# Reciprocals of the softmax row sums spread over partitions through a DRAM row, in an attention and soft-mixture kernel

## What is computed

```python
q = (x @ Wq).reshape(B, N, HEADS, DIM_HEAD)          # x: [8, 56, 128], layer-normed
k = (context @ Wk).reshape(B, M, HEADS, DIM_HEAD)    # context: [8, 1500, 128]
v = (context @ Wv).reshape(B, M, HEADS, DIM_HEAD)
attn = softmax(einsum('bihd,bjhd->bhij', q, k) * SCALE)
x = x + einsum('bhij,bjhd->bihd', attn, v).reshape(B, N, INNER) @ Wo
# then, on layernorm(x):
logits = (einsum('tzd,ed->tze', x, phi_w) + phi_b).reshape(t, z, n, p)
D, C = softmax(logits, axis=3), softmax(logits, axis=2)
X_tilde = tanh(norm(clip(einsum('tznp,tzd->npd', D, x))))
Y_tilde = einsum('npd,ndH->npH', X_tilde, expert_w) + expert_b
out = x + einsum('tznp,npH->tzH', C, Y_tilde)
```

## Time and profile before

| | |
|---|---|
| three runs | 484.78, 487.85, 488.55 us; median 487.85 us |
| profiled execution | span 483.5 us from its first to its last instruction; no other time of it is given |
| PE busy | 441.9 us (91%), weight loads 384.6 us (80%) |
| DVE busy | 359.2 us (74%) |
| ACT busy | 256.8 us (53%) |
| POOL busy | 120.6 us (25%) |
| chain that ended last | PE 69%, DVE 22%, DMA 4%, ACT 3% of the span |

### The profile page before, as it was taken

How to read it: one execution, slowest core, us unless ns; L and a number is a source line. 1 busy time by engine, 2 the same in 40 slices (tenths; PEclk the granted TensorE clock), 3 DMA queues, 4 the chain that set the end, 5 groups by cost and what they waited for, 6 DMA issues and landing times.

```text
span 483.5 us, 7391 instructions
## 1 busy us (share of the span) xinstructions
PE 441.9 (91%) x2776; PEld 384.6 (80%) x2776; DVE 359.2 (74%) x600; ACT 256.8 (53%) x439; POOL 120.6 (25%) x55
## 2 busy tenths in 40 slices
PE   2899899999999999999999999999999995865767
PEld 2788788898899889988988897889878875565657
DVE  2467776777786777768666877675799999999780
ACT  1466566665564556656565565663666640325532
POOL 0507000503050022305000503050123428434250
PEclk9999999999999999999999999999999999778899
DMA  7110100010010001000100021000000009800000
GB/s 214 42 64 1 66 1 0 1 65 0 2 42 24 1 0 66 0 0 2 61 0 0 30 85 37 1 1 1 0 2 0 1 0 276 159 0 2 1 1 20
DMA packets 8496, 15.38 MB, mean 32 GB/s; under 512 B 291, under 2 KB 4275, under 8 KB 8469
## 3 DMA queue, kind: packets, MB, share of 16 engines
q1 hardware_dynamic: 6996, 12.91, 9.2%
q10 hardware_dynamic: 1472, 2.10, 1.5%
HBM read 14.78 MB, written 0.23 MB: 31 GB/s over the span
## 4 chain that ended last, share of the span: by engine, by line
PE 69%; DVE 22%; DMA 4%; ACT 3%; issue 1%; POOL 0%; SPq 0%; DVEq 0%
PE turned L575 14%; PE scores L563 7%; PE scores L565 7%; PE scores L564 7%; PE acc L593 7%; PE acc L595 7%; PE acc L594 7%; DVE csum L1359 3%; PE misc L507 3%; DMA ctx_raw<-in_ctx_dram 3%; DVE bankmax L1290 3%; DVE cmax L1342 2%; DVE pT_l L1299 2%; PE misc L609 2%; PE misc L501 2%; DVE disp L1377 2%
## 5 line engine op out<-in xcount | busy, mean ns | idle before, releaser
L1299 DVE TENSOR_TENSOR pT_l<-turned,pT_h 125x512 fp32r<-125x512 f32 x168 | 112.2, 688 | 65.8 <-ACT pT_h L1019 65.3
L1019 ACT CAST pT_h<-turned 125x512 fp32r<-125x512 f32 x168 | 95.3, 592 | 112.6 <-PE turned L575 112.4
L1290 DVE TENSOR_REDUCE bankmax<-scores 128x1 f32<-128x500 f32 x168 | 110.5, 675 | 20.6 <-PE scores L565 20.3
L575 PEld LDWEIGHTS turned<-ident,prob 128*125 128x125 f32 x672 | 88.3, 187 | 14.7 <-DVE pT_l L1299 8.5
L575 PE MATMUL turned<-ident,prob 128*125 128x128 f32 x672 | 94.4, 276 | 2.4 <-DVE pT_l L1299 2.2
L1026 ACT ACTIVATE prob<-scores,negmax 128x1500 f32<-128x1500 f32 x56 | 85.1, 1520 | 9.9 <-DVE negmax L1293 9.8
L593 PE MATMUL acc<-pT_h,ctx_nh 125*128 125x384 f32 (+1 forms) x192 | 78.2, 407 | 0.0
L595 PE MATMUL acc<-pT_h,ctx_nl 125*128 125x384 f32 (+1 forms) x192 | 70.1, 365 | 0.0
L594 PE MATMUL acc<-pT_l,ctx_nh 125*128 125x384 f32 (+1 forms) x192 | 69.9, 364 | 0.0
L563 PE MATMUL scores<-ctx_th,qk_h 128*128 128x500 f32 x168 | 69.2, 412 | 0.6 <-DVE qk_l L1283 0.3
L385 POOL TENSOR_TENSOR ctx_nh<-ctx_raw,zero 125x1536 fp32r<-125x1536 f32 x8 | 22.0, 2748 | 184.4 <-PE acc L595 169.3
(11 more groups left out here) (169 smaller groups left out, 581.1 us busy)
## 6 DMA issues: line engine op xcount, KB each, us to landing
ctx_raw<-in_ctx_dram SPq DMA_DIRECT2D x7, 750.0 KB
eb<-in_L_ffn_expert_b_dram SPq DMA_DIRECT2D x4, 256.0 KB, 8.0
ctx_raw<-in_ctx_dram SPq DMA_DIRECT2D x3, 250.0 KB
wq_sb<-in_L_xattn_Wq_dram ACTq DMA_DIRECT2D x1, 512.0 KB, 5.2
wk_sb<-in_L_xattn_Wk_dram ACTq DMA_DIRECT2D x1, 512.0 KB, 8.6
wv_sb<-in_L_xattn_Wv_dram ACTq DMA_DIRECT2D x1, 512.0 KB, 9.1
wo_sb<-in_L_xattn_Wo_dram ACTq DMA_DIRECT2D x1, 512.0 KB, 15.0
x_sb<-in_x_dram SPq DMA_DIRECT2D x1, 224.0 KB, 5.7
```

The costliest lines, as they stand in the source:

```text
L575: last = tr(turned[0:CK, m, 128 * c:128 * c + 128], prob[u][:, CK * j:CK * j + CK], ident[:, :])
L1019: nc.scalar.copy(pT_h[0:CK, t, CPB * k:CPB * k + CPB, :], turned[0:CK, (KB * u + k) % 2, :].rearrange("p (c r) -> p c r", c=CPB)).then_inc ...
L1290: m = v.tensor_reduce(bankmax[:, u, k:k + 1], scores[:, k, 0:KW], AX.X, ALU.max)
L1299: v.tensor_tensor(pT_l[0:CK, t, dst, :], turned[0:CK, (KB * u + k) % 2, :].rearrange("p (c r) -> p c r", c=CPB), pT_h[0:CK, t, dst, :].bit ...
```

## The change

`spread_rden` and its wait go from PE, `copy_rbc` goes from ACT. In their place SP has a `spread_rden` of two DMAs: the first writes the reciprocals of the group from `rden` into a row in DRAM, element by element in the order (row, tile); SP waits for its landing and for the `normalise` before, and the second reads the row back, broadcast to the 128 partitions of `rbc`. `normalise` waits for that DMA and reads `rbc` with a step of 3 or 4 elements, since the tile index is now the fastest. SP's loop is written out. PE's waits that leaned on `copy_rbc` lean on other semaphores that have come by then.

```diff
+            def spread_rden(n, a, grp):
+                t0, t1 = GROUPS[grp]
+                w = t1 - t0
+                row = rden_row[grp].rearrange("r t -> (r t)")[0:128 * w]
+                sp.wait_ge(rden_dve, n)
+                sp.dma_start(row.rearrange("(r t) -> r t", t=w), rden[:, a * NT + t0:a * NT + t1]).then_inc(rden_out, 16)
+                sp.wait_ge(rden_out, 16 * n)
+                wait(sp, oT_dve, n - 1)
+                sp.dma_start(rbc[:, 0:128 * w], row.partition_broadcast(128)).then_inc(rbc_in, 16)
+
+            def half(b, a, first=False):
+                if not first:
+                    spread_rden(2 * b, 1 - a, 1)
+                load_ctx(b + 2)
+                spread_rden(2 * b + 1, a, 0)
+
             load_ctx(1)
-            with sp.Fori(1, PAIRS) as i:
-                load_ctx(2 * i)
-                load_ctx(2 * i + 1)
+            half(0, 0, first=True)
+            half(1, 1)
+            for i in range(1, LAST):
+                half(2 * i, 0)
+                half(2 * i + 1, 1)
+            spread_rden(2 * (B - 2), 1, 1)
             sp.wait_ge(qk_pe, 4 * PAIRS)
             sp.dma_start(phi_sb[:, :, :], phi_w.rearrange("(k p) d -> p k d", p=128)).then_inc(phi_in, 16)
...
+            spread_rden(2 * (B - 2) + 1, 0, 0)
+            spread_rden(2 * (B - 1), 0, 1)
+            spread_rden(2 * B - 1, 1, 0)
+            spread_rden(2 * B, 1, 1)
             sp.wait_ge(pv_pe, 2 * B)
             sp.dma_start(ew[:, :, :], expert_w.rearrange("n d h -> d n h")).then_inc(ew_in, 16)
...
-            def spread_rden(a, grp, m):
-                t0, t1 = GROUPS[grp]
-                for t in range(t0, t1):
-                    last = tr(misc[:, m, 128 * (t - t0):128 * (t - t0) + 128],
-                              rden[:, a * NT + t:a * NT + t + 1].broadcast_to([128, 128]), ident[:, :])
-                last.then_inc(rbc_pe, 1)
...
-            def copy_rbc(n, grp, m):
-                act.wait_ge(rbc_pe, n)
-                wait(act, oT_dve, n - 1)
-                w = 128 * (GROUPS[grp][1] - GROUPS[grp][0])
-                nc.scalar.copy(rbc[:, 0:w], misc[:, m, 0:w]).then_inc(rbc_act, 1)
...
             def normalise(n, a, grp):
-                dve.wait_ge(rbc_act, n)
+                dve.wait_ge(rbc_in, 16 * n)
                 dve.wait_ge(pv_pe, n)
                 t0, t1 = GROUPS[grp]
-                w = 128 * (t1 - t0)
-                v.tensor_tensor(oT_cols[:, a, 128 * t0:128 * t1], acc[:, 0:w], rbc[:, 0:w],
+                w = t1 - t0
+                v.tensor_tensor(oT_cols[:, a, 128 * t0:128 * t1].rearrange("p (t r) -> p t r", t=w),
+                                acc[:, 0:128 * w].rearrange("p (t r) -> p t r", t=w),
+                                rbc[:, 0:128 * w].rearrange("p (r t) -> p t r", t=w),
                                 ALU.mult).then_inc(oT_dve, 1)
```

More of the change, by code:

```diff
@@ L150, in xattn_softmoe_kernel @@
         rden, _ = take("rden", [128, 2 * NT])
+        rden_row = nc.dram_tensor("rden_row", [2, 128, 4], F32, kind="Internal").ap()
         assert place[0] <= nc.sbuf_usable_end
@@ L232, in xattn_softmoe_kernel @@
         rden_dve = sem("rden_dve")
-        rbc_pe = sem("rbc_pe")
-        rbc_act = sem("rbc_act")
+        rden_out = sem("rden_out")
+        rbc_in = sem("rbc_in")
         oT_dve = sem("oT_dve")
@@ L649, in early @@
                 if step == (0, 0, True):
-                    pe.wait_ge(rbc_act, 2 * b - 1)
+                    pe.wait_ge(qk_lo, 4 * PAIRS - 1)
                     pe.wait_ge(y_act, 2)
@@ L660, in early @@
                 if step == (0, 2, True):
-                    pe.wait_ge(rbc_act, 2 * b)
+                    pe.wait_ge(x1_dve, 1)
                     turn_phi(2, M0)
@@ L682, in early @@
                 if step == (1, 0, False):
-                    pe.wait_ge(rbc_act, 2 * b - 1)
+                    pe.wait_ge(logit_act, 2)
                     logits(0, 3)
@@ L688, in early @@
                 if step == (1, 2, True):
-                    pe.wait_ge(rbc_act, 2 * b)
+                    pe.wait_ge(logit_act, LC)
                     logits(1, 0)
@@ L791, in half @@
                         make_qk(i + 1, 0, 0)
[L792 to L797, removed]
                     if 2 <= t <= 4 and not last and not first:
@@ L802, in half @@
                         elif k == 1:
-                            wait(pe, rbc_act, b * 2)
+                            pe.wait_ge(ctxT_lo, KB * b + 3)
                         elif a == 0:
@@ L822, in half @@
                         project(0)
[L823 to L835, removed]
+                    if t == 6 and a == 0 and not first:
+                        project(1).then_inc(y_pe, 1)
                     if ending:
@@ L880, in _ @@
             turn_probs(G - 1, 1, 1)
-            pe.wait_ge(logit_act, 2 * LC + 3)
-            pe.wait_ge(rden_dve, 2 * B)
-            spread_rden(1, 1, 1)
             turn_probs(G - 1, 1, 2)
@@ L886, in _ @@
             context_product(B - 1, 1, 1, range(CPB, NC), by_bank=True)
+            pe.wait_ge(logit_act, 2 * LC + 3)
             logits(2, 3)
@@ L895, in _ @@
             slots_in(0, 1)
-            pe.wait_ge(rbc_act, 2 * B)
             slots_in(0, 2)
@@ L1148, in half @@
                         hi_qk(i + 1, 0, 0)
-                    if t == 1 and not first:
-                        copy_rbc(b * 2, 1, a)
                     if 2 <= t <= 4 and not last and not first:
@@ L1154, in half @@
                         hi_qk(i + 1, t - 3, (t - 3) % 2)
[L1155 to L1158, removed]
+                    if t == 6 and a == 0 and not first:
+                        copy_y(i - 1)
                     if ending:
@@ L1181, in _ @@
             hi_probs(G - 1, 1, NT - 1, 2)
-            copy_rbc(2 * B, 1, 1)
             dispatch_exp(1)
```

## The result

The changed kernel takes 493.95 us (median of four runs, 493.09 to 495.68) against 486.56 us (four runs, 484.78 to 488.55) for the kernel before: a ratio of 1.0155, 95% interval 1.0118 to 1.0192. The profiled execution has a span of 492.4 us, against 483.5, and a time of 494.22 us. It is slower, by 8.9 us between the two spans. The four executions of the kernel before lie 3.8 us apart, and eleven and seventeen further ones have medians of 487.65 and 487.47 us; against those the change is 6.3 to 6.5 us.

A forecast was written before the change was run, and what follows sets the result against it. PE was taken to bound the kernel until 369.76 us, then mostly DVE. The terms -4.9 + 9.8 + 2.7 + 0.7 = +8.3 us on the median of 487.85 gave 496.2 us, range 491 to 501.

The forecast's parts named there:

- What leaves PE: Groups of transposes gone from PE: fourteen before 369 us save 4.9 us, the last two counted at nothing.
- The price by starts: A transpose group on PE costs how much later the next scores start: 0.44, 0.25 or 0.33 us.
- The full lengths: Rival: PE gets back each transpose's recorded 272 ns, 13.3 us in all, kernel at 485.3 us; chance 0.08.
- What is moved on SP: Load of phi_w queued behind step 12's DMAs: PE stands still 9.8 us more before turn_phi(0), range 8.6 to 10.9.
- The clock: Behind PE's stall at turn_phi(0), PE works at 1.2 GHz for a while: 2.7 us lost, from 2.2 to 3.2.
- The stepped read: normalise on DVE reads rbc with a step of 12 or 16 bytes: 0.7 us more, from 0 to 1.8.
- The trip in the loop: Reciprocals' write to DRAM and read back: some 4.8 us, between 3.4 and 8.4, hidden by 12 us or more.
- The rival of the long trip: At step 15 a trip over 5.9 us makes DVE wait before normalise: 2.0 us more, 498.2 us; chance 0.10.

The follow-up runs named there:

- e1: Changed kernel with the load of phi_w issued in front of step 12's two DMAs again, as in the kernel before; 480.99 us, ratio 0.9897.
- e2: Kernel before, with one wait added so SP issues the load of phi_w only after step 12's reciprocals; 497.27 us, ratio 1.0203.
- e3: Changed kernel with 100 extra transposes of the identity on PE in front of the wait for phi_w; 492.16 us, ratio 1.0134.
- e5: On top of e1, the load of phi_w cut in two, the part turn_phi(0) reads first; 480.99 us, ratio 0.9867 to the kernel before.
- e4: On top of e1, the DRAM row laid out by tile, so normalise reads without a step; 502.6 us, ratio 1.0331 to the kernel before.

## Why the prediction was right

The forecast was 8.3 us more, 496.2 us. Between the spans it was 8.9 us, from step 1 on 8.6. The median moved by 7.4, to 493.95, inside the range of 491 to 501. The forecast was counted from a median before of 487.85 us in three runs; with one run more it was 486.56, with eleven and seventeen 487.65 and 487.47.

The mechanism was right: the late load and the lower clock behind it. That the sum came within 0.6 us is in part luck, since its errors cancel: the stall was 1.7 us longer than forecast and outside its own range of 8.6 to 10.9, while the clock and the stepped read together cost 1.2 us less.

- **What leaves PE**: forecast 4.9 us for fourteen groups, of which 5 x 0.44 + 4 x 0.25 + 0.33 = 3.53 us are between the marks of steps 1 and 11. Measured there 3.50, in e1 3.46. The price by starts was right in the sum, and the 0.44 stands in the rows above. It was not spread quite as forecast: each of the four halves from step 3 to 11 is 0.76 us shorter, not 0.69, and the stretch from step 1 to 3 only 0.45, not 0.77. So a group at the end of a t = 6 was worth 0.32; behind a `project` it is 2.33 us from that one's start to the second score matmul before (239.58 to 241.91) and 2.01 after (237.09 to 239.10). Why the first stretch gave less is open. The full lengths would have given 9.5.
- **What is moved on SP**: forecast 9.8 us more of standing still, measured 12.96 - 1.47 = 11.5. The mechanism was right in each link, and shown by e1 (load in front, loss gone) and e2 (load late, loss there). Two sizes were off: the write of step 12 took 3.1 us where I had 1.8, and from the broadcast's issue to the load's it was 0.5 where I had 0.3. My range for the write, 1.2 to 2.4, did not hold step 12, although it held most other steps. The load of `phi_w` with the broadcast in front of it took 6.9 us, as forecast (6.44 + 0.6). The Trainium skill ("DMA: Bandwidth & Descriptors", Anatomy of one DMA), whose section is on DMAs issued by GpSimd while these are issued by SP, has some 2.0 us fixed, and says that the delay can be surprisingly long when the target is HBM. Here the writes took 1.4 to 3.1 us, so some lie below that figure and step 12 above it.
- **The clock**: forecast 2.7 us, measured 2.2 by e3, the lower end of the bounds from the pauses in the mixture, 2.2 to 3.2. The Trainium skill ("TensorE: Matmul & The Clock Gate", What's actually happening) has under 1% of a typical kernel for the ramp; 2.2 us are 0.4% of this one, so the figure holds, and they are still a quarter of the net change.
- **The stepped read**: forecast 0.7 us; in the loop nothing of it shows. The operation itself is at its dearest end, 1.06 us for 512 elements, 0.39 more than before. The cover held: DVE's 0.19 us of slack was used up, and the row maxima behind the slower `normalise` ran a little faster (1.85 us instead of 2.02; they start later against the scores, so that the last bank is there when they come to it), so PE's wait stayed at 0.24 us:

```profile
264.39 1.09 DVE L1302 TENSOR_TENSOR oT<-acc,rbc 128x512 f32<-128x512 f32 x1
...
265.40 1.85 DVE L1275 TENSOR_REDUCE bankmax<-scores 128x1 f32<-128x500 f32 x3
...
267.39 0.69 DVE L1284 TENSOR_TENSOR pT_l<-turned,pT_h 125x512 fp32r<-125x512 f32 x1
...
268.13 0.51 PEld L599 LDWEIGHTS turned<-ident,prob 128*125 128x125 f32 x4 [0.24 <-DVE pT_l L1284]
```

- **The trip in the loop**: forecast 4.8 us, measured 1.4 to 3.1 for the write and 3.4 to 4.4 for the read, together 5.0 to 6.7. The read was too low at 2.7. The loop hid it, as forecast. The rival of the long trip was nearer than its chance of 0.10 says: step 15's broadcast was issued at 392.44 us, took 3.8, and `normalise` started at 396.30, without a wait; in e5 it did wait, 0.22 us.

By account of the stretch from step 11 to 16: 11.5 of waiting, 2.2 of clock, less 2 x 0.44 + 2 x 0.32 = 1.5 for the groups of steps 11 to 14, is 12.2 us; measured 12.4. The 0.2 us are missing in e1 too (0.5 more of waiting less 1.5 is 1.0 shorter, measured 0.8), and no run shows where they go; the stepped reads of these steps may have them.

## What to carry to other kernels

A DMA that waits for another engine makes everything behind it on its issuing queue wait too, so before one is put into a queue, list what stands behind it and ask when each of those is needed; here one load of 1 MB that was 1.5 us late decided the sign. Keep loads that a compute engine waits for in front of round trips, or cut off the piece that is needed first. And price what is taken from a busy PE by the starts of its neighbours in the timeline, and add a low-clock stretch to a stall as long as these (9 to 13 us of an idle PE cost 1.6 to 2.2 us more; the 2 us in e1 cost none).

## What was not expected of the hardware

- The reciprocals' write of 1.5 KB in pieces of 12 bytes landed later than that of 2 KB in pieces of 16 bytes, in 2.1 against 1.4 us in the median, also at steps 13 and 15, where no context load is in front of it. Pieces of 4 bytes took about 8 us for the same bytes. Step 12, in pieces of 16, took 3.1, 2.7 and 2.2 us in the changed kernel, e3 and e1, where its equals took 1.4 (step 4: 1.6 to 1.9). In e5 step 12 took 1.4 like the others. Why remains open; a PE that stands still is not the cause, nor the late load, since e1 has neither.
- A step of 16 bytes in one SBUF operand cost DVE 0.39 us for 512 elements, the same 0.76 ns an element as a step of 128 bytes; a step of 12 bytes cost 0.11 us for 384, or 0.29 ns an element. In e4, which differs in `normalise` by this step alone, both are back at 0.67 and 0.55 us. The Trainium skill ("SBUF — State Buffer", Door 1: The DMA port swizzle) has lines of 16 bytes and calls a stride of up to four fp32 free; for this operation four was at the full price and three at a third of it, and the measurement decides.
- The eight profiled executions fall into two groups before step 1: three reach it at 59.6 to 60.3 us and five at 62.7 to 63.6. In the profiled execution of e1 PE's setup products near 20 us are recorded at 0.42 us each, in that of the kernel before, near 19 us, at 0.27 us, and at step 1 e1 is 3.0 us behind:

```profile
19.32 0.42 PE L547 MATMUL acc<-wkT,wqT 64*128 64x128 f32 x1
...
21.97 3.75 PE L531 MATMUL misc<-xnT,wqk 128*128 128x112 f32 x16
```

The corresponding sixteen matmuls in the kernel before:

```profile
20.41 2.01 PE L507 MATMUL misc<-xnT,wqk 128*128 128x112 f32 x16 [0.28 <-issue]
```

The clock rows show 1.00 for this stretch in both, so that this is a lower clock is a guess from the longer durations. Three microseconds are more than half of the 4.3 that e1 gains from step 1 on, which is why stretches were compared and not spans.
